# A grouped convolution between two expert layers: from 8-position blocks by batch to 16-position blocks with both batches in one operand

## The reference, cut to what matters

```
def reference(x, cond, ...):                       # x: (64, 64, 1024) fp32, cond: (64, 128)
    x = x + ffn0(cond0(x, cond))                   # cond0: per batch a 64x64 mix over channels;
                                                   # ffn0: 1024x1024 layer, router (top 2 of 8), LoRA experts
    x = x + ffn1(conv1(x, cond))
    return x

def conv1(x, c):                                   # x: (batch, 64 channels, 1024 positions)
    out = conv1d(x, weight, padding=4, groups=4)   # 9 taps, 16 channels in and 16 out per group
    return out + (c @ c_weight.T)[:, :, None] + bias[None, :, None]

def ffn1(x):                                       # softmax over 8 experts of q.k, LoRA experts, 1024x1024 layer
    q, k, h = x @ Wq.T, x @ Wk.T, x @ A
    return x @ W.T + b + (softmax(q.k / sqrt(32)) * h) @ Bm
```

## Time and profile before

| | before |
|---|---|
| median of 3 runs | 1286.98 us (1285.96 to 1288.63) |
| the profiled execution's own time | 1286.87 us |
| its span | 1285.1 us |
| TensorE busy | 1275.6 us (99%), 7210 matmuls |
| VectorE busy | 715.1 us (56%) |
| ScalarE busy | 280.4 us (22%) |
| GpSimd busy | 240.6 us (19%) |
| groups 1365 and 1366 (convolution, tiles 1 to 31) | 117.4 and 110.6 us busy, x496 each |

### The profile page before, as it was taken

How to read it: one execution, slowest core, us unless ns; L and a number is a source line. 1 busy time by engine, 2 the same in 40 slices (tenths; PEclk the granted TensorE clock), 3 DMA queues, 4 the chain that set the end, 5 groups by cost and what they waited for, 6 DMA issues and landing times.

```text
span 1285.1 us, 20731 instructions
## 1 busy us (share of the span) xinstructions
PE 1275.6 (99%) x7210; PEld 1189.1 (93%) x7210; DVE 715.1 (56%) x1728; ACT 280.4 (22%) x516; POOL 240.6 (19%) x174
## 2 busy tenths in 40 slices
PE   8999999999999999999999999999999999999998
PEld 8999999999999998899889889889988988988997
DVE  6787877767778777544434443444443443344432
ACT  6323332222322334211111111111111111111110
POOL 2344522332322330010001001001000100100100
PEclk9999999999999999999999999999999999999999
DMA  8245433334333357424223323322423322332310
GB/s 306 92 133 168 153 108 114 122 121 125 107 112 111 106 197 234 119 90 120 69 86 113 78 69 108 100 69 91 117 69 87 116 74 69 109 99 69 95 43 33
DMA packets 83879, 141.55 MB, mean 110 GB/s; under 512 B 6657, under 2 KB 52097, under 8 KB 83841
## 3 DMA queue, kind: packets, MB, share of 16 engines
q1 hardware_dynamic: 83840, 141.06, 36.5%
HBM read 88.59 MB, written 52.45 MB: 110 GB/s over the span
## 4 chain that ended last, share of the span: by engine, by line
PE 92%; DVE 4%; DMA 2%; issue 1%; POOL 1%; ACT 0%; SPq 0%; DVEq 0%; POOLq 0%
PE ps L1221 28%; PE ps L1223 27%; PE ps L1222 27%; PE ps L1365 6%; PE ps L1366 2%; DMA row<-spill 1%; POOL mixw L589 1%; DMA staging<-in_w 0%; DMA xo<-in_xt 0%; DVE weights L888 0%; DVE row L921 0%; PE ps L1341 0%; PE ps L1459 0%; DVE mix_hl L898 0%; DVE part L913 0%
## 5 line engine op out<-in xcount | busy, mean ns | idle before, releaser
L1221 PE MATMUL ps<-weights,lhs_h 128*128 128x512 f32 (+2 forms) x1408 | 498.4, 354 | 0.8 <-issue 0.8
L1223 PE MATMUL ps<-weights,lhs_l 128*128 128x512 f32 (+2 forms) x1408 | 490.2, 348 | 0.0
L1222 PE MATMUL ps<-weights,lhs_h 128*128 128x512 f32 (+2 forms) x1408 | 489.1, 347 | 0.0
L1221 PEld LDWEIGHTS ps<-weights,lhs_h 128*128 128x128 f32 x1408 | 264.8, 188 | 23.9 <-issue 1.1
L1223 PEld LDWEIGHTS ps<-weights,lhs_l 128*128 128x128 f32 x1408 | 264.4, 188 | 20.8
L1222 PEld LDWEIGHTS ps<-weights,lhs_h 128*128 128x128 f32 x1408 | 264.8, 188 | 20.1
L653 POOL TENSOR_TENSOR xo<-row,wsum 128x512 f32<-128x512 f32 x60 | 76.8, 1305 | 660.4 <-DMA out_x<-xo 660.4
L1221 PE MATMUL ps<-weights 128*128 128x396 f32 x384 | 132.1, 344 | 1.3 <-DVE weights L888 1.3
L1222 PE MATMUL ps<-weights 128*128 128x396 f32 x384 | 131.5, 342 | 0.0
L1223 PE MATMUL ps<-weights 128*128 128x396 f32 x384 | 131.5, 342 | 0.0
L1193 DVE TENSOR_TENSOR xo<-ps,xo 128x512 f32<-128x512 f32 x64 | 43.1, 691 | 149.7 <-PE ps L1223 149.7
(11 more groups left out here) (156 smaller groups left out, 1434.0 us busy)
## 6 DMA issues: line engine op xcount, KB each, us to landing
row<-spill SPq DMA_DIRECT2D x30, 576.0 KB, 4.4
z<-x_round SPq DMA_DIRECT2D x64, 256.0 KB, 5.3
xo<-in_xt SPq DMA_DIRECT2D x31, 512.0 KB, 3.9
out_x<-xo SPq DMA_DIRECT2D x31, 512.0 KB, 2.7
x_round<-row SPq DMA_DIRECT2D x60, 256.0 KB, 2.1
row<-in_xr SPq DMA_DIRECT2D x31, 394.0 KB, 3.4
spill<-row SPq DMA_DIRECT2D x31, 394.0 KB, 4.3
staging<-in_w SPq DMA_DIRECT2D x8, 832.0 KB, 7.0
```

The lines of the kernel that those rows point to most:

```text
L1221: pe.matmul(out_ap, lhs[0], rhs[0], start=first, stop=False, skip_group_check=True)
L1222: pe.matmul(out_ap, lhs[0], rhs[1], start=False, stop=False, skip_group_check=True)
L1223: return pe.matmul(out_ap, lhs[1], rhs[0], start=False, stop=last, skip_group_check=True)
```

## The change

For tiles 2 to 31 the stationary operand is 64 blocks of 16 positions of one group for each of the two batches, (batch, block), 128 columns. Three windows w = 0, 1, 2 of z, each with a step of two blocks, take the place of m = 0, 1, and conv(t, h) does two groups for both batches in place of four groups of one batch. Window 1 meets both output octets of the 16 positions (512 columns with the high part, 256 with the low), windows 0 and 2 one each (256 and 128). PSUM partitions are then (batch, block of 16), columns (octet, part, 8 positions x 16 channels). conv_read_low sorts them back into whole by sixteen instructions of 64 partitions x 256 columns; the order of the partitions there becomes (octet, block), and w1 is laid out to fit. The split operands no longer fit in the tile part and lie in twelve pieces (sets, last_set) in part, mix_hl and ones. Tiles 0 and 1 keep the multiplication by batch (by_batch), but z is split for them too in windows, into the runs of runs01, hw_hl and mix_hl among them. conv_hl holds its two bands in the other order. Semaphores z_hi and z_lo count 24 a tile, conv_part and conv_read 8. The first weight piece is loaded and split as two of 396 columns each (pieces0), so all later pieces have their numbers one higher, and SyncE issues one DMA more before cpack.

```diff
+        sets = [part[:, n // 4, n % 4 * 256:n % 4 * 256 + 256] for n in range(8)] + \
+               [mix_flat[:, n * 256:n * 256 + 256] for n in (1, 2, 3)]
+        last_set = [ones[:, :], part[:, 0, 1024:1024 + P]]
...
+        def z_blocks(w):
+            return z[:, :, :].rearrange("p (b g) w -> p b g w", b=2)[:, :, :, w:w + P - 1:2]
...
-        pieces0 = [(0, 0, 2), (0, 2, 4), (0, 4, 6), (0, 6, 8), (1, 0, 4), (1, 4, 8), (2, 0, 4), (2, 4, 8)]
+        pieces0 = [(0, 0, 1), (0, 1, 2), (0, 2, 4), (0, 4, 6), (0, 6, 8), (1, 0, 4), (1, 4, 8), (2, 0, 4), (2, 4, 8)]
...
             sp.dma_start(xo[:, 0, 0:512], a["xt"][0:P, 0:512]).then_inc(first_in, 16)
             chunk(0)
+            chunk(1)
             sp.dma_start(xo[:, 0, 512:D], a["xt"][0:P, 512:D]).then_inc(xt_in[0], 16)
-            chunk(1)
+            chunk(2)
             sp.dma_start(cbuf[:, 0:CPACK], a["cpack"]).then_inc(cond_in, 16)
...
                 for h in range(2):
-                    if h == 0:
-                        act.wait_ge(z_in, t * 32 + 32)
-                        if later(t, 2):
-                            act.wait_ge(conv_done, t * 2)
-                    q = slice(GRP * h, GRP * h + GRP)
-                    act.activation(high[:, q, 0:W], z[:, q, :], ACT.Copy).then_inc(z_hi, 1)
+                    if by_batch(t):
+                        for g, flat in runs01[t][0, h]:
+                            run = flat.rearrange("p (g w i) -> p w g i", w=3, i=64)
+                            n = run.shape[2]
+                            for w in range(3):
+                                act.activation(run[:, w], z_blocks(w)[:, h, g:g + n], ACT.Copy).then_inc(z_hi, n)
+                        continue
+                    for w in range(3):
+                        act.activation(sets[h * 3 + w].rearrange("p (g b i) -> p b g i", g=2, b=2),
+                                       z_blocks(w)[:, :, 2 * h:2 * h + 2], ACT.Copy).then_inc(z_hi, 4)
...
+                    for w in range(3):
+                        dve.wait_ge(z_hi, t * 24 + h * 12 + w * 4 + 4)
+                        n = 6 + h * 3 + w
+                        high = sets[h * 3 + w].rearrange("p (g b i) -> p b g i", g=2, b=2)
+                        if n < len(sets):
+                            dve.tensor_tensor(sets[n].rearrange("p (g b i) -> p b g i", g=2, b=2),
+                                              z_blocks(w)[:, :, 2 * h:2 * h + 2], f32(high),
+                                              ALU.subtract).then_inc(z_lo, 4)
+                            continue
+                        for g in range(2):
+                            dve.tensor_tensor(last_set[g].rearrange("p (b i) -> p b i", b=2),
+                                              z_blocks(w)[:, :, 2 * h + g], f32(high[:, :, g]),
+                                              ALU.subtract).then_inc(z_lo, 2)
...
-                    dve.tensor_tensor(dst, part[0], add[:, :, None, :].to_broadcast([P, GRP, J, GC]),
-                                      ALU.add).then_inc(conv_part, 1)
-                    dve.wait_ge(conv_part, t * 2 + h + 1)
-                    dve.tensor_tensor(dst, part[1], dst, ALU.add).then_inc(conv_read, 1)
...
+                    for b in range(2):
+                        for k in range(2):
+                            q, to = slice(64 * b, 64 * b + 64), slice(64 * k, 64 * k + 64)
+                            dve.tensor_tensor(where_to[to, b], parts[q, :, k, 0],
+                                              add[to, b, :, None, :].to_broadcast([64, 2, J, GC]),
+                                              ALU.add).then_inc(conv_part, 1)
+                    dve.wait_ge(conv_part, t * 8 + h * 4 + 4)
+                    for b in range(2):
+                        for k in range(2):
+                            q, to = slice(64 * b, 64 * b + 64), slice(64 * k, 64 * k + 64)
+                            dve.tensor_tensor(where_to[to, b], parts[q, :, k, 1], where_to[to, b],
+                                              ALU.add).then_inc(conv_read, 1)
...
+                for g in range(2):
+                    dst = ps[:, (BP1, BP0)[h][g], :].rearrange("p (k s n) -> p k s n", k=2, s=2)
+                    both = conv_hl[:, :, 2 * h + g, :, :]
+                    for w, out_k, rows in ((1, slice(0, 2), slice(0, 2)), (0, slice(0, 1), slice(1, 2)),
+                                           (2, slice(1, 2), slice(0, 1))):
+                        pe.matmul(dst[:, out_k], stationary(t, 0, h, g, w), both[:, rows], start=(w == 1), stop=False,
+                                  skip_group_check=True)
+                        mm = pe.matmul(dst[:, out_k, 0, :], stationary(t, 1, h, g, w), both[:, rows, 0, :], start=False,
+                                       stop=(w == 2), skip_group_check=True)
```

More of the change, by code:

```diff
@@ L1100, in conv_read_low @@
                     pair0 = (BP1, BP0)[h][0]
-                    parts = ps[:, pair0:pair0 + 2, :].rearrange("p k (g s n) -> p (k g) s n", g=2, s=2)
-                    part = [parts[:, :, s].rearrange("p g (r o) -> p g r o", r=J) for s in range(2)]
-                    dst = whole[:, :, 64 * h:64 * h + 64].rearrange("p r (g o) -> p g r o", g=GRP)
-                    add = bias_in[:, u, 64 * h:64 * h + 64].rearrange("p (g o) -> p g o", g=GRP)
-                    dve.tensor_tensor(dst, part[0], add[:, :, None, :].to_broadcast([P, GRP, J, GC]),
-                                      ALU.add).then_inc(conv_part, 1)
@@ L1107, in conv_read_low @@
-                    dve.wait_ge(conv_part, t * 2 + h + 1)
-                    dve.tensor_tensor(dst, part[1], dst, ALU.add).then_inc(conv_read, 1)
+                    if by_batch(t):
+                        parts = ps[:, pair0:pair0 + 2, :].rearrange("p k (g s n) -> p (k g) s n", g=2, s=2)
+                        part0, part1 = (parts[:, :, s].rearrange("p g (r o) -> p g r o", r=J) for s in range(2))
+                        dst = whole[:, :, 64 * h:64 * h + 64].rearrange("p r (g o) -> p g r o", g=GRP)
+                        add = bias_in[:, u, 64 * h:64 * h + 64].rearrange("p (g o) -> p g o", g=GRP)
+                        dve.tensor_tensor(dst, part0, add[:, :, None, :].to_broadcast([P, GRP, J, GC]),
+                                          ALU.add).then_inc(conv_part, 4)
+                        dve.wait_ge(conv_part, t * 8 + h * 4 + 4)
+                        dve.tensor_tensor(dst, part1, dst, ALU.add).then_inc(conv_read, 4)
+                        continue
@@ L1112, in conv_read_low @@
[L1112 to L1113 removed]
+                    dve.tensor_tensor(tokens_of(t, lhs_l[:, u], h), tokens_of(t, whole, h),
+                                      f32(tokens_of(t, lhs_h[:, u], h)), ALU.subtract).then_inc(cv_lo, 1)
             y_low(T3, 0)
@@ L1355, in conv @@
             def conv(t, h):
-                high, low = (z0h, z0l) if at(t, 0) else (zh, zl)
-                pe.wait_ge(z_lo, t * 2 + 1 + h)
+                pe.wait_ge(z_lo, t * 24 + h * 12 + 12)
                 if h == 1 and before_end(t, 1):
                     pe.wait_ge(x1_ready, t * 2 + 4)
-                for g in range(GRP):
-                    b = GRP * h + g
-                    dst = ps[:, (BP1, BP0)[h][g // 2], (g % 2) * 256:(g % 2) * 256 + 256]
-                    for m in range(2):
-                        both = conv_hl[:, m, g, :, :].rearrange("p s n -> p (s n)")
-                        pe.matmul(dst, high[:, b, m:m + P], both, start=(m == 0), stop=False, skip_group_check=True)
-                        mm = pe.matmul(dst[:, 0:P], low[:, b, m:m + P], conv_hl[:, m, g, 0, :], start=False,
-                                       stop=(m == 1), skip_group_check=True)
+                if by_batch(t):
+                    for g in range(GRP):
+                        dst = ps[:, (BP1, BP0)[h][g // 2], (g % 2) * 256:(g % 2) * 256 + 256]
+                        for m in range(2):
+                            both = conv_hl[:, 1 - m, g, :, :].rearrange("p s n -> p (s n)")
+                            pe.matmul(dst, stationary(t, 0, h, g, m), both, start=(m == 0), stop=False,
+                                      skip_group_check=True)
+                            mm = pe.matmul(dst[:, 0:P], stationary(t, 1, h, g, m), conv_hl[:, 1 - m, g, 0, :],
+                                           start=False, stop=(m == 1), skip_group_check=True)
+                    mm.then_inc(conv_done, 1)
+                    return
```

140 lines of the change are left out of this document (88 added, 52 removed).

## The result

| | before | after |
|---|---|---|
| median of 4 runs each | 1286.92 us (1285.96 to 1288.63) | 1276.75 us (1275.14 to 1277.15) |
| ratio, with 95% interval | | 0.9917 (0.99 to 0.9934) |
| profiled execution: own time, span | 1286.87, 1285.1 us | 1277.15, 1275.4 us |

The change makes the kernel 10.2 us (0.8%) faster. The forecast was 12.7 us, 1274.2; the time lies inside the range, above the forecast. The page and the whole list of what TensorE waited for come first, as in the earlier trace rows (columns of the second: total us, times, longest).

The account below looks back on a forecast made before the run. TensorE's own instruction stream was taken as the bound, busy 1275.6 of 1285.1 us. The sum was 1286.87 - 13.8 (Part 1) + 0.9 (Part 4) + 0.2 (Part 5) = 1274.2 us, range 1271.5 to 1281.0, forecast 75%.

Parts of the forecast that it names:

- Part 1: Convolution in blocks of 16 positions, tiles 2 to 31: 8 weight loads fewer, 0.46 us less a tile, 13.8 in all.
- Part 2: VectorE's reading of the convolution result: four instructions become sixteen, 0.455 us each; 2.2 us left before TensorE asks, no cost.
- Part 3: Splitting z: ScalarE's two copies become six (2.0 us), VectorE's two instructions seven (2.3 us); no cost in steady tiles.
- Part 4: Tiles 0 and 1, z split in more instructions: +0.5 and +0.4 us, together +0.9, from 0 to 2.5.
- Part 5: First weight piece in two, at the start: the wait only moves; +0.2 us, from -0.3 to +0.6.
- rival A: Convolution: printed starts are true, a 256-column product behind a short one costs 0.17 us; 1280.5 us in all, 12%.
- B: Convolution: cost goes by columns, 6144 a tile before and after; 1288.0 us in all, 6%.
- C: Convolution: products in two runs are slow; at double cost for eight a tile, 1315.3 us in all, 4%.
- D: VectorE's sixteen reads become the bound: from 0.59 us each TensorE waits at hw_low; at 0.91, some 1440 us, 3%.

Follow-up runs that it names:

- the convolution alone: The changed kernel with the first weight piece in one again, all else as changed: 1275.34 us, run once more 1275.63 us.
- the gap filled: The changed kernel with five more products on constants between the first two steps of the first product and cond(0): 1276.44 us, ratio 0.9909.

## Why the prediction was right, and where it was off

**The bound: right.** TensorE's own stream sets the end. The second phase shows no wait of it, before or after, and 0.41 us less of its stream a tile came out as time.

**Part 1: right in its count, a tenth too large.** A half took 1.61 and 1.62 us where 1.60 to 1.62 were forecast and 1.84 stood before, so the convolution gives back 0.45 to 0.46 a tile as said; the run with 64 columns shows that instructions are what counts there and columns aren't. But the tile is 0.41 shorter, not 0.46. The rest is in the products around the convolution, which I had taken as unchanged: from the second 512-column product behind the second half to the transpose it is 1.86 us (807.39 to 809.25) where the trace of before has 1.83, and over a whole tile the distances of the 110 other products sum to 21.15 us for 21.11. Why they take 0.04 more wasn't tested; four more reads of PSUM by VectorE a tile leave the period as it is (24.28). 30 x 0.05 = 1.5 us of the forecast gain.

**Part 2: right.** Length 0.42 and distance 0.453, for 0.425 and 0.455; nothing overlaps. The slack is 2.5 us for 2.2 forecast, and the runs with more reads agree: 3.62 us of reads cost 1.1 a tile.

**Part 3: right, at the lower bound.** The seven of z_low take 2.2 us (813.10 to 815.26) for 2.3 forecast, ScalarE's six 2.08 for 2.0: a stride of two costs nothing here. The row in section 5.2 of "Vector Engine (DVE) Microarchitecture Reference" of the Trainium skill that I drew on is for a source that hops 4 KiB at every element; for a stride of two elements, with the other source dense, this trace doesn't show such a price. (By that row and my line the seven would have taken some 3.3 us, not 3.5.)

**Part 4: right in place, and within its bounds in this trace.** z_low(0) takes 2.5 us for 2.6 forecast and ends at 490.7, for 488.3 to 488.6; 2.4 of that is the lag of the whole trace by then (VectorE, to be held against the earlier trace rows):

```profile
488.17 1.70 DVE L1142 TENSOR_TENSOR weights<-z,weights 128x256 fp32r<-128x256 f32 x6 [2.02 <-ACT weights L847]
489.79 0.50 DVE L1142 TENSOR_TENSOR hw_hl<-z,weights 128x64 fp32r<-128x64 f32 x3
490.20 0.49 DVE L1142 TENSOR_TENSOR mix_hl<-z,weights 128x64 fp32r<-128x64 f32 x3
...
507.23 3.45 DVE L1142 TENSOR_TENSOR part<-z,part 128x256 fp32r<-128x256 f32 x6
...
511.22 3.68 DVE L936 TENSOR_TENSOR weights<-staging,weights 128x1664 fp32r<-128x1664 f32 x2
```

```profile
506.72 2.75 POOL L695 TENSOR_TENSOR xo<-biased,wsum 128x512 f32<-128x512 f32 x2 [23.77 <-DMA spill<-xo]
```

TensorE's wait for the tokens of tile 0 grew from 0.78 to 1.06 us, and from 469 us to the start of tile 0 the lag grows by 0.3 us (0.2 in the change run again; 0.65 and 0.9 with the convolution alone). z_low(1) beside GpSimd is as slow as the split of the earlier trace rows, so the last two weight pieces end at 514.90 only and TensorE's first product with the last of them starts at 514.95, 0.27 late; in the other traces of the changed convolution that is 0 to 0.7. Between the two, 0.2 is given back: the trace of before waits 0.4 us for tmpw at 504.23, that of after doesn't. Together the lag grows by 0.4 us here. In four other traces of the changed convolution it is 0.4 to 0.7, but 1.4 with four more reads and 2.5 with the gap filled, for 0.9 forecast with 2.5 as the bound. One bound was worked out wrongly: z_low(0) has 3 x 256 + 3 x 128 + 6 x 64 = 1536 elements and not 1024, so at the worst rate of part 3 it would have taken 5.1 us and not 3.4. It didn't come near.

**Part 5: the step that failed.** I costed it at +0.2 and at most +0.6. The profile shows +2.0 behind 78 us, and the medians +1.1 to +1.4 in the changed kernel, +0.9 with at most 1.2 by the interval in the old one. Three terms were wrong. The landing: I wrote that the wait moves "unless a transfer is issued later by one more entry on SyncE's queue", and that is what the diff does, an entry more ahead of cpack; I had the condition and 0.43 us for the issue, but took +0.2 for the whole part. It is 0.48 us for the issue and 0.4 for the longer transfer. The slack at 78 us: I spoke only of what TensorE gains ahead of it, and counted on it for what comes late too; it takes up 0.6 us where least is late (1.20 to 0.60 in the run with cpack one place later, 0.86 to 0.26 in that with the gap filled), and 0.4 and next to nothing in the two traces of the change. And the clock, which the text didn't weigh: TensorE has its first products sooner, runs out of them sooner, stands for a second or more, and in most executions then runs at 1.2 GHz for some 3.4 us. That is 1.6 us of the profiled 2.44 at 29 us, and 1.4 us by the runs of the split alone at either mean clock.

The sum in the profile is then: -12.4 by the period, +0.4 where the phases meet, +0.4 around 405 us, +2.0 at the start, together -9.6 for the -9.7 of the spans. The +0.4 at the end of the first phase's loop, a wait put down to "issue" that grows from 0.2 to 0.6 us, is in all traces of the changed convolution and of others between -0.2 and +0.6, and I have no cause for it. Against the forecast's -12.7 these terms are 1.4 us short in part 1, 1.8 over in part 5, 0.4 unforeseen at 405 us and 0.5 under in part 4, which by luck takes a little back. The range, drawn wide for rival A, took the rest in.

**Rivals.** A and B fall by the halves of 1.61 and 1.62 and by the 64-column run. C falls by the starts behind the two-run products. "Advanced Engine Details and Errata" of the Trainium skill, PSUM Cachelines, says that any non-contiguous pattern slows matmuls significantly; for runs of 128 words this trace doesn't agree (0.12 us to the next start). D didn't happen, but it is real beyond 2.5 us.

**What stays open.** Why the clock rises before 5 us in one execution and near 7 in another of the same start, and falls again in some. With the split and no filler it fell in three of the five executions profiled, without the split in none of six; by the mean clocks the split makes it frequent, but what in it does so isn't shown, since cpack one DMA later alone, in its single execution, kept the clock. Open too is what spreads the runs at a mean clock of 1.000, 1285.46 to 1289.91 us in the kernel before. One part of it may be the transfers where the phases meet.

## What to carry to other kernels

Where TensorE is the bound and its products are short, count instructions, each with its weight load, and not columns: 240 products fewer at the same number of columns gave 12.4 us, and halving the columns of the short ones gave none. VectorE may take over the sorting, even at two and a half times its former time there, as long as the transfer that TensorE waits for last still ends in time; work out that slack, since from its end on each microsecond is paid in every tile. And an earlier first product is worth nothing if the data for the next ones don't come earlier too: here one more DMA ahead of them made cond(0) 0.8 us late, and the medians are 1.1 to 1.4 us higher.

## What the runs showed of the hardware

- A matmul of 128 stationary columns in float32r costs about 0.115 us at least, the distance of the weight loads: with 64 instead of 128 moving columns the pair of products keeps 0.23 us and the kernel its time (1.0005). Whether the load itself or another fixed cost sets it wasn't separated.
- TensorE's clock near the start differs from execution to execution: the same warming products took 0.95 or 1.49 us for three. After a wait of 1.0, 1.1 and 1.4 us it fell to 1.2 GHz for some 3.4 us, after one of 2.3 us, in a kernel with the same start, it didn't. An execution with the low stretch takes about 1.4 us more (1288.4 and 1287.0). Up to its first fall the profile's clock column stands at 1.00, whatever the durations say.
- VectorE's instructions that change the partition half follow each other with a gap of 0.03 us (0.422 long, 0.453 apart), where those in place overlap by 0.08.
- A source with a stride of two costs VectorE and ScalarE nothing: two 128x256 subtractions take 0.75 us, six copies 2.08. Beside GpSimd the same subtractions are far slower: the six at 507.23 (three of 256 columns, three of 128) take 3.45 us, six of the same widths at 488.17 take 1.70. GpSimd worked from 506.72 to 509.47 and the first two of the six ran in that time, at 1.07 and 1.52 us in place of 0.42; the other four took their usual time.
